# A four-block graph network on one core: preparation of the edges rebuilt, degrees of two chunks sent ahead of x

## What is computed

```python
h = jnp.maximum(_layernorm(x, axis=-1), 0.0)
x = x + _L0_gnn_ref(h, edge_index, ...)   # sum over edges, (1 + eps) h, two dense layers, log_softmax
...                                       # L1: two graph convolutions, scaled by 1/sqrt(degree)
...                                       # L2: four layers of edge sum, two dense layers, batch norm
...                                       # L3: powers of the normalised adjacency, batch norm, dense layers

# within L0, the first of them:
aggr = jax.ops.segment_sum(x[src], dst, num_segments=N_NODES)
h = (1.0 + eps) * x + aggr
h = jax.nn.relu(h @ W1 + b1)
h = h @ W2 + b2
```

## Time and profile before

| | us |
|---|---|
| median of three runs | 1236.78 |
| the profiled execution | 1235.06 |
| its span | 1233.5 |
| TensorE busy | 1130.0 (92%) |
| VectorE busy | 683.1 (55%) |
| ScalarE busy | 452.3 (37%) |
| GpSimd busy | 11.8 (1%) |
| mean granted TensorE clock | 0.978 of full speed |

### The profile page before, as it was taken

How to read it: one execution, slowest core, us unless ns; L and a number is a source line. 1 busy time by engine, 2 the same in 40 slices (tenths; PEclk the granted TensorE clock), 3 DMA queues, 4 the chain that set the end, 5 groups by cost and what they waited for, 6 DMA issues and landing times.

```text
span 1233.5 us, 19328 instructions
## 1 busy us (share of the span) xinstructions
PE 1130.0 (92%) x6308; PEld 658.9 (53%) x6308; DVE 683.1 (55%) x2170; ACT 452.3 (37%) x1339; POOL 11.8 (1%) x37
## 2 busy tenths in 40 slices
PE   1677899999799999999899899998699999999997
PEld 1556667666464464644545445445455456544644
DVE  8999999996454225545346264345545334632311
ACT  1557998896464112211311311312422113820100
POOL 1000000000000000000000000000100000000000
PEclk9999899999899999999999899999899999999999
DMA  3100000001101013524133133299922213510001
GB/s 70 28 2 1 2 2 10 2 2 30 25 3 26 17 30 66 110 58 91 32 77 74 37 72 80 56 228 197 233 65 67 87 50 85 133 38 25 12 25 30
DMA packets 208150, 70.32 MB, mean 57 GB/s; under 512 B 180944, under 2 KB 207126, under 8 KB 208048
## 3 DMA queue, kind: packets, MB, share of 16 engines
q1 hardware_dynamic: 119840, 41.90, 15.2%
q10 hardware_dynamic: 87840, 25.80, 9.6%
q0 software_dynamic: 368, 1.34, 0.6%
HBM read 20.71 MB, written 28.26 MB: 40 GB/s over the span
## 4 chain that ended last, share of the span: by engine, by line
PE 80%; DVE 11%; DMA 3%; ACT 2%; issue 2%; SPq 1%; ACTq 1%; DVEq 0%; POOL 0%; POOLq 0%
PE PS L1182 50%; PE PS L891 7%; DVE HPb L755 4%; PE PS L2574 4%; PE PS L1541 3%; PE PS L880 2%; PE PS L856 2%; PE PS L2043 2%; PE PS L2049 2%; DVE HPb L706 2%; DMA HPb<-deg_d 1%; PE PS L1658 1%; PE PS L2081 1%; DMA Zf<-di_d 1%; PE PS L1227 1%
## 5 line engine op out<-in xcount | busy, mean ns | idle before, releaser
L1182 PE MATMUL PS<-ADJ,HPb 125*128 125x500 bf16 (+2 forms) x2250 | 450.0, 355 | 0.1
L1182 PEld LDWEIGHTS PS<-ADJ,HPb 125*128 125x128 f16 x2250 | 219.2, 98 | 224.2 <-issue 33.5
L927 ACT CAST ADJ<-PS 126x72 f32 (+7 forms) x784 | 193.2, 315 | 51.6 <-PE PS L891 18.4
L1182 PE MATMUL PS<-ADJ,Zf 125*128 125x500 bf16 (+2 forms) x1050 | 202.1, 352 | 0.0
L891 PE MATMUL PS<-HPb 128*128 128x150 bf16 (+3 forms) x784 | 191.6, 346 | 3.5 <-ACT ADJ L927 2.5
L1182 PEld LDWEIGHTS PS<-ADJ,Zf 125*128 125x128 f16 x1050 | 102.4, 97 | 93.8 <-issue 1.3
L755 DVE TENSOR_SCALAR HPb<-XRf,Zf 128x176 bf16<-128x176 f16 (+2 forms) x588 | 134.7, 289 | 1.3 <-PE PS L891 0.7
L880 PEld LDWEIGHTS PS<-HPb 128*128 128x128 bf16 x642 | 86.1, 141 | 59.7 <-issue 34.2
L1842 DVE CUSTOM_DVE_ANT_0 HPb<-ADJ,HPb 125x625 bf16<-125x625 bf16 x125 | 101.2, 809 | 3.7
L880 PE MATMUL PS<-HPb 128*128 128x25 bf16 x642 | 90.5, 214 | 12.9 <-DVE HPb L755 12.0
L1944 DVE TENSOR_SCALAR Zf<-PS,B_L 128x500 f32<-128x500 f32 (+2 forms) x28 | 19.1, 682 | 138.7 <-PE PS L2049 138.7
(11 more groups left out here) (336 smaller groups left out, 1094.9 us busy)
## 6 DMA issues: line engine op xcount, KB each, us to landing
adj_d<-ADJ ACTq DMA_DIRECT2D x25, 700.0 KB
HPb<-y_d SPq DMA_DIRECT2D x19, 187.5 KB, 2.7
HPb<-di_d SPq DMA_DIRECT2D x10, 250.0 KB, 3.5
adj_d<-ADJ ACTq DMA_DIRECT2D x25, 81.2 KB
ADJ<-in_x SPq DMA_DIRECT2D x1, 1562.5 KB
q_d<-HPb SPq DMA_DIRECT2D x25, 62.5 KB
HPb<-di_d SPq DMA_DIRECT2D x5, 305.2 KB
HPb<-s_d ACTq DMA_DIRECT2D x5, 250.0 KB, 3.8
```

Source lines behind the costliest of these rows:

```text
L927: e.copy(to, WPS[group % BANKS][0:PD, t0 * RESTS[q]:t1 * RESTS[q]] .rearrange("p (t d) -> p t d", t=t1 - t0)).then_inc(s_mv, 1)
L1182: mm = e.matmul(accs[q], H[0:PN, t, q, 0:P], cols, start=(t == 0 and (two or q == 0)), stop=(t == NT - 1 and (two or q == 1)), skip_group_ ...
```

## The change

It has four parts.

1. **Start of the engines.** Only the last 256 columns of partitions 96 to 127 are padded, and SyncE waits for that only before the last two loads; the two constants of `base_d` are sent right behind the loads. GpSimd writes its ramps and constants first and adds to the semaphores afterwards. VectorE casts the ramps ahead of the bound for the L1 weights, and the scaling of these weights moves to the end of VectorE's L0. TensorE's wait for it moves into L1's `outputs(0)`. The DMAs of all other weights move from ScalarE's queue to SyncE's, behind x.
2. **The chain on VectorE.** Tables have 98 partitions. Division rounds by adding and subtracting 1.5 * 2^23, with no correction. The shift by the group's first destination goes to ScalarE; `til_f` is released first, then `src_f`, then `key_f`. The sort test is one instruction. Copies to f16 and to `IOC` go to ScalarE.
3. **Transposes.** Each half of a table has a PSUM bank of its own, and each table is begun when it is ready.
4. **Degrees.** Chunks 0 and 1 go out together. SyncE brings chunk 0 back, then chunk 1, then loads x for 17 tiles, then sends the other degrees and the factors of chunk 0.

The diff, cut to its core (`WHOLES` is 1.5 * 2.0 ** 23; the code of GpSimd is the old one with the semaphore loop moved below its second `sem_inc`):

```diff
+                e.wait_ge(s_pad, 4)
+                for dram_t, tile in ((a["dst"], dst_i), (a["src"], src_i)):
+                    e.dma_start(tile[q0:q0 + 1, padded][:, 0:E - FULL * GE], ...).then_inc(s_in, 16)
+                e.dma_start(base_d[G + 1:G + 2]..., FL[0:1, 3:4]).then_inc(s_base, 16)
+                e.dma_start(base_d[0:1]..., FL[0:1, 2:3]).then_inc(s_base, 16)
             if act:
                 ...
+                e.wait_ge(s_pad, 4)
+                e.copy(TMP[0:1, 0:1], FL[0:1, 2:3].bitcast(F32)).then_inc(s_null, 1)
+                e.wait_ge(s_rows, 1)
+                for k in range(KR):
+                    e.activation(t3[:, k, :], d3[:, k, :], ACT.Identity, bias=ST[0:QG, 0, k:k + 1]).then_inc(s_rowc, 1)
             if dve:
+                e.memset(dst_i[q0:P, padded], N).then_inc(s_pad, 1)
+                e.memset(src_i[q0:P, padded], PAD_SRC).then_inc(s_pad, 1)
                 ...
+                e.wait_ge(s_const, 1)
                 ...
+                e.wait_ge(s_w1, 48)
                 ...
+                line(e.tensor_scalar(INV[:, :], P3[:, 0:P], 1 / TOP, 1e-30, ALU.mult, ALU.max))
+                e.wait_ge(s_in, 16 * n_in)
+                line(e.tensor_copy(dst_f, dst_i[0:QG]))
+                line(e.tensor_scalar(ST[0:QG, 0, 0:KR], d3[:, :, 0], -1.0, None, ALU.mult))
+                e.sem_inc(s_rows, 1)
+                line(e.tensor_copy(src_f, src_i[0:QG]))
+                line(e.tensor_scalar(key_f, src_f, -(PN - 1) / 2.0, 1.0 / PN, ALU.add, ALU.mult))
+                line(e.tensor_scalar(key_f, key_f, WHOLES, -WHOLES, ALU.add, ALU.add))
+                e.wait_ge(s_rowc, KR)
+                for k in range(KR):
+                    line(e.scalar_tensor_tensor(out=t3[:, k, :], in0=k3[:, k, :], scalar=float(WINS[k]), in1=t3[:, k, :], ...))
+                e.sem_inc(s_rows, 1)
+                line(e.scalar_tensor_tensor(out=src_f, in0=key_f, scalar=-float(PN), in1=src_f, ...))
+                e.sem_inc(s_rows, 1)
+                line(e.scalar_tensor_tensor(out=key_f, in0=dst_f, scalar=float(NT), in1=key_f, ...))
+                e.sem_inc(s_rows, 1)
                 ...
                 e.wait_ge(s_base, 96)
                 ...
-                line(e.tensor_tensor(cmp3[:, :, 0:GE - 1], d[:, :, 0:GE - 1], d[:, :, 1:GE], ALU.is_gt))
-                for k in range(KR):
-                    line(e.tensor_reduce(flags[:, k, 0:1], cmp3[:, k, 0:GE - 1], AX.X, ALU.add))
+                line(e.tensor_tensor_reduce(out=cmp3[:, :, 0:GE - 1], in0=d[:, :, 0:GE - 1], in1=d[:, :, 1:GE], scale=1.0,
+                                            scalar=0.0, op0=ALU.subtract, op1=ALU.max, accum_out=flags[:, 0, 0:1]))
+                e.sem_inc(s_frow, 1)
                 ...
-                line(e.tensor_copy(IOC, IOP.rearrange("p (n o) -> p n o", o=1).broadcast_to([P, P, HC])))
                 e.wait_ge(s_fsum, 1)
-            tables = ((KT, til_f, 2), (PT, src_f, 3), (KGT, key_f, 4))
+            tables = ((KT, til_f, (2, 0)), (PT, src_f, (3, 1)), (KGT, key_f, (6, 7)))
             if pe:
+                    e.wait_ge(s_rows, n + 2)
-                        if h:
-                            e.wait_ge(s_rowc, 2 * n + 1)
             if act:
+                    if n == 1:
+                        for h in range(GC):
+                            e.copy(PTH[:, 0:NCH]..., PS[:, banks[h], 0:G]).then_inc(s_rowc, 1)
+                e.wait_ge(s_frow, 1)
+                e.copy(IOC, IOP.rearrange("p (n o) -> p n o", o=1).broadcast_to([P, P, HC])).then_inc(s_rowc, 1)
                 def part_a():
-                    e.wait_ge(s_rowc, 6)
-                    line(e.tensor_copy(PTH[:, 0:NCH], PT))
+                    e.wait_ge(s_rowc, KR + 9)
             def degree_landed(c, p):
-                return 16 * (2 + p + (c > 0) * (1 + DG + (1 + DG) * (c - 1)))
+                return 16 * (2 + p + DG * c + (c if c > 1 else 0))
-                        e.dma_start(deg_d[:, cols]..., ADJ[PN:PD, :, cols])
+                        two = slice(0, (nt + SPANS[1][1]) * PN)
+                        e.dma_start(deg_d[:, two]..., ADJ[PN:PD, :, two])
-                    if c == 0:
-                        rest = slice(nt * PN, N)
-                        e.dma_start(deg_d[:, rest]..., ADJ[PN:PD, :, rest])
+                    if c == 1:
                         for v, j, n in ((XRf[:, 8 * P:], 8, 7), (Zf[:, 3 * NCH + 2 * P:], 15, 1), (XRf[:, 16 * P:], 16, 9)):
                             e.dma_start(v[0:PN, 0:n * P]..., xt[:, j:j + n, :]).then_inc(s_x, 16)
-                    elif c < NC - 1:
+                        rest = slice((j0 + nt) * PN, N)
+                        e.dma_start(deg_d[:, rest]..., ADJ[PN:PD, :, rest]).then_inc(s_dt, 16)
+                    if 0 < c < NC - 1:
                         di_out(c - 1, s_dt)
                 normed(NC - 2, NC - 1)
                 e.sem_inc(s_dout, 1)
+                line(e.reciprocal(GAT[:, 0:P], INV[:, :]))
+                line(e.tensor_tensor(WL1[:, 1], WL1[:, 1], GAT[:, 0:P], ALU.mult))
+                line(e.tensor_scalar(WL1[:, 1], WL1[:, 1], LOW, None, ALU.mult))
+                e.sem_inc(s_sc[2], 1)
                 def outputs(c):
+                    if c == 0:
+                        e.wait_ge(s_sc[2], 1)
-                e.wait_ge(s_sc[2], 1)
```

149 lines of the change are left out of this document (65 added, 84 removed).

## The result

The changed kernel takes **1223.06 us** (median of 4 runs, 1222.06 to 1226.15) where the kernel before took 1236.36 beside it (4 runs, 1235.34 to 1237.25): a ratio of 0.9897, interval 0.9877 to 0.9917. That is 13.3 us won where 21.9 were forecast (1236.36 less the 1214.5 of the forecast), and outside the range given. The profiled execution has a span of 1221.1 us against 1233.5.

A forecast was written before the change was run, and what follows sets the result against it. Bounds: the start (GpSimd, VectorE's edges, transposes) to 35 us and SyncE's queue of degrees at 292 to 318. Gains 14.2 + 7.8 = 22.0 off 1235.06 gave 1213.1, as median 1214.8; 1214.5 was taken, range 1210.5 to 1220.5.

The forecast's parts named there:

- Later chunks keep their distance of some 14 us: Degrees: after chunk 2, the later chunks' degrees were taken to stay some 14 us ahead, with no new stall.
- chunk 2's stall: Degrees: chunk 2's land at 327.0, TensorE asks at 325.8, so 1.2 us returns and 7.8 are won.
- the 1.3 and 15.6 us: Degrees, after chunk 1's at 303.6: 1.3 us to the first packet, 15.6 for the data, then 4.9 for the factors.
- the second rival: Degrees of chunk 2 late: TensorE idles 3 us or more, falls to 1.2 GHz, 3 to 4 won there, 1219; chance 0.15.
- the rival's 3 us: Degrees of chunk 2: idle time of 3 us or more, behind which TensorE's clock falls to 1.2 GHz; chance 0.15.
- 12.1 for 14.2: Start: first one-hots at 20.7 instead of 34.85, 14.2 us won, bounds 15.0 and 9.4.
- the bound of 8.3: Start: edges begin on VectorE at 7.5; 8.3 at the latest if the edges' loads slow the L1 weights.
- 6.05 for 5.7: Start: from the pointers to the first one-hots, 9.4 us before, 5.7 left after the removed steps.
- the 3.8 between 2.3 and 5.70: Start: write of 392 single-element pointers lands in 3.8 us, between 25 elements in 2.3 and 500 in 5.70.
- The Trainium skill's 2.0 us: A DMA's fixed cost of about 2.0 us, by which the rival without any wait (1212.5, chance 0.10) would hold.
- far bound of 19.8: Start: latest time for the pointers to be ready, if their write is as slow as before; forecast 15.0.
- Chunk 1's stall and its low clock: Degrees of chunk 1: TensorE's 6.58 us idle and 2.44 us of slow matmuls both go, 9.0 us.

The follow-up runs named there:

- after_again: The changed kernel run once more, unaltered, for a second profile: 11.4 us won over the kernel before.
- own_count: The changed kernel with the factors' write counted on a semaphore of its own, so the next degrees no longer wait for its landing: 1215.85 us.
- weights_act: own_count with the other layers' weight loads issued again by ScalarE at the start, not by SyncE behind x: time within the expected 1218 to 1220 us.
- degrees_only: The kernel before with only the new order of the degrees' transfers: 1229.41 us.
- no_bound: own_count without the bound for the L1 weights at the start (INV is ones, so results are wrong): 2.8 us longer than own_count by the ratios.
- rows_390: own_count with factors written one chunk later and base_d filled from input dst in memory as 390 elements and one: first one-hots at 24.04 us.
- start_only: The changed kernel with the degrees' transfers in the order of before: 1224.26 us.
- filled_dst_first: The changed kernel with factors counted apart and written one chunk later, dst loaded first, and five unused tiny memsets on VectorE: 0.9805 of before.

## Why the prediction was wrong

**The degrees, the main miss.** Two steps failed. The first is "Later chunks keep their distance of some 14 us": in the kernel before, the way back of chunk 3's degrees was issued 13.5 us ahead of their use (335.34 against 348.86), but that of the last chunk's only 2.7 (373.88 against 376.62). They are sent for only when the factors of the chunk before have landed, 6.9 to 7.4 us after their issue, and TensorE waits for them (1.48 us in the changed kernel, and with the clock behind it, 11.26 for 9.81, a lead that falls from 17.0 to 14.25; in after_again it falls from 14.6 to 9.35). In the kernel before, this same chain was just hidden, as TensorE's timeline shows:

```profile
376.62 0.24 PE L1507 MATMUL PS<-SM,HPb 25*125 25x1 bf16 x2 [0.34 <-DMA HPb<-deg_d]
```

Its landing of 5.70 stood in the earlier trace rows; who waited for it was not followed. The second is a term that was right in kind: chunk 2's stall was forecast at 1.2 and came at 1.73. Its sum holds for the most part: 21.8 us were worked out from chunk 1's degrees to the landing of the factors, and 21.2 were measured (293.97 to 315.14); no row shows the 1.3 and 15.6 us into which it is split, but own_count has the rest of the degrees told 17.2 us after chunk 1's (293.30 to 310.46) where they make 16.9. The way back took 2.60 and not 1.6. But the stall had been priced as if it were stable. It was 1.73 in one profile of the changed kernel and 3.43 in the other, in part by the landing of a few hundred single elements, and behind the 3.43 the 34 matmuls took 8.86: what the second rival describes, to which 0.15 was given. Its cause was not quite the rival's: the last to land were the factors, and the rest of the degrees some 5 us before them (own_count). Nor do the runs bear out the rival's 3 us: at the last chunk the clock was 0.72 behind a stall of 1.48. own_count, which takes the factors' landing out of both places, recovers 8.4 to 9.9 us.

**The start, 2.1 us short (12.1 for 14.2).** By its terms: the edges 1.06 late, as the L1 weights landed at 5.56 beside the edges' loads and not at 4.45 (the bound of 8.3 had this cause and was too low; 8.16 to 8.83 in the other four profiles with this start); VectorE's own chain 7.4 for 7.2; the write of the pointers 6.3 for 3.8, mended in part by read-backs of 3.4 for 4.3, so that the wait was 0.68 for 0.3; from pointers to one-hots 6.05 for 5.7. The choice that failed is the 3.8 between 2.3 and 5.70, taken nearer to the small end "because the 392 spread over more transfer engines". They do not land sooner for it. The Trainium skill's 2.0 us (same page, Anatomy of one DMA, where it is fitted to transfers issued by GpSimd; these are SyncE's) would have been further off still: the writes of 392 to 500 single elements in these traces took 5.7 to 7.4 us with nothing large beside them, and 8.5 beside the weights (weights_act); in before and degrees_only, where two more small writes follow, all three were told 9.2 and 12.6 us after the first was issued. The prediction's far bound of 19.8 was itself 0.6 short, as 6.85, the 9.24 of before and 4.3 make 20.4. The error in the 3.8 cost only 0.4 us, because the error on VectorE's side was almost as large: the two paths end together, as no_bound and rows_390 show from their two sides.

**Between, 2.5 us that no step had.** The lead falls from 12.1 to 9.7 during the build. About 0.8 of it goes in the first twelve halves, as in all kernels that keep the changed kernel's list of VectorE instructions, in steps of 0.2 to 0.35. The rest, 1.7, goes together with a lower clock; TensorE in three stretches, first of before, then of after:

```profile
108.00:116.00 8.00, 6.79 (x56) 0.80 0.01 3
...
124.00:132.00 8.00, 6.69 (x53) 0.79 0.01 2
...
140.00:148.00 8.00, 6.77 (x54) 0.79 0.01 3
```

```profile
108.00:116.00 8.00, 7.28 (x52) 0.57 0.01 3
...
124.00:132.00 8.00, 7.69 (x50) 0.50 0.01 3
...
140.00:148.00 8.00, 7.79 (x53) 0.60 0.00 0
```

The granted clock is 0.79 to 0.80 in before and 0.50 to 0.60 in this execution of after, where TensorE is busy for more of each stretch with no more matmuls (own_count has 0.86, 0.79 and 0.72). From 90 to 160 us the clock is 0.83 in after and 0.93 in after_again, which loses 0.3 us in place of the 1.7; own_count has 0.85 and loses 0.5. So the loss differs from execution to execution, no experiment changed it on purpose, and why the clock stayed low is not shown.

**The way to the end, 2.1 us that no step had either.** Of it 1.0 us goes at 585 to 592 us, together with the clock: TensorE is busy for 1.1 of the 5 us from 580, in before for 1.0 of the 5 from 594, and in the 5 us that follow the granted clock is 0.50 in after and 0.66 in before. after_again has 0.50 there too and loses 1.6 us; start_only has 0.75 and loses nothing. 0.5 us goes in the stage with the two waits.

**What held.** No wait for ScalarE's shifts; `IOC` done (18.56 plus 1.68) before the first one-hots needed it; the flag test 0.5 us behind the flags; the weights behind x free, with no wait for them at the second part (and worth 5.0 us in front of the pointers, by weights_act); the moved L1 steps free: VectorE still idles for 3.64 us behind them. Chunk 1's stall and its low clock went as worked out.

The sum, on the profiled execution: 22.0 less 2.1 at the start, 2.4 in the build, 0.4 at chunk 2, 2.8 at the last chunk and 2.1 from there to the end makes 12.2; the two spans differ by 12.4. The range missed it because its far end allowed for only one thing going wrong, and because the build, the last chunk and the way to the end were taken to pass a gain on whole. The forecast's own remark that what is won arrives at the end "unless something takes over" had no number.

**The best version** is not the changed kernel but dst_first, which is it with the factors counted apart and written one chunk later and `dst` loaded first: 0.9803 [0.9790, 0.9817] of before, 24.7 us; filled_dst_first (0.9805) can't be told from it.

## What to carry to other kernels

When a stall is removed, follow every small transfer on the same queue to the work that waits for it, at the last chunk as well as at the next one, and ask how many tenths of a us it was hidden by. A count shared by two kinds of transfers makes the slower one a gate for the faster; a count of its own was worth 8.4 to 9.9 us here, beside 11 to 13 for the whole change. Where two paths end together, shortening one is worth nothing, and an error in the price of the longer one is not found until the other is short.

## What was not expected of the hardware

- A write of single 4-byte elements to memory is told late: 392 elements in 6.3 to 7.1 us, 500 in 5.7 to 7.4, with nothing large beside them, where the last read-back of the 392 takes 2.0 to 2.8.
- 391 single elements from memory to memory took about 20 us; with 390 of them the loads behind them were in 1.6 to 3.6 us after their issue. One issue of the slow kind kept two later loads of 640 bytes waiting until 25 us.
- A read that itself takes 1.7 us is told after 5.36 if a slow small write was issued before it.
- Five instructions that do nothing, put where the engine waits, went together with losses of 0.3 to 0.85 us at other halves of the build, 36 to 78 us into the kernel, in one profile of each of two kernels.
